# A mixture-of-experts loop: the down product with the inner rows stationary, and no transposes behind it

## What is computed

```python
E, K, H, F = (64, 6, 256, 96)
CAP = 2 * (2 * 128 * K // E)          # 48
...
buf = jnp.zeros((E, CAP + 1, H), x.dtype).at[se, slot].set(x[tok])[:, :CAP]
h = jax.nn.silu(jnp.einsum('ech,ehf->ecf', buf, w_gate)) * jnp.einsum('ech,ehf->ecf', buf, w_up)
out = jnp.einsum('ecf,efh->ech', h, w_down)
gathered = out[se, jnp.minimum(pos, CAP - 1)] * valid.astype(x.dtype)[:, None]
w = topk_w.reshape(-1)[order].astype(x.dtype)[:, None]
return jax.ops.segment_sum(gathered * w, tok, num_segments=Tn)
```

## Time and profile before

| | |
|---|---|
| three runs | 491.72, 495.5, 497.8 us (median 495.5) |
| the profiled execution | 492.98 us |
| its span in the trace | 491.0 us |
| mean granted PE clock | 0.921 of 2.4 GHz |
| expert loop in the trace, first `gate_up` to last scatter matmul | 179.12 to 304.96 us |

### The profile page before, as it was taken

The page is one execution under the profiler, slowest core; times in us unless marked ns, Lnnn a source line. Parts: engine busy times, 40 slices in busy tenths (PEclk is TensorE's granted clock), DMA queues, the critical chain, the costliest instruction groups (busy, mean ns, idle before and its releaser), DMA issues.

```text
span 491.0 us, 5331 instructions
## 1 busy us (share of the span) xinstructions
PE 417.0 (85%) x1778; PEld 245.5 (50%) x1778; DVE 374.3 (76%) x691; ACT 220.6 (45%) x411; POOL 96.0 (20%) x65
## 2 busy tenths in 40 slices
PE   0695999987970589999999999999999989998672
PEld 0241564576830246788888887544444434433220
DVE  4999788987799865988867785931796976739995
ACT  4464636382261355665666647152101104035880
POOL 0000000000000174222100000004768456541000
PEclk9998677998995698999999888799999999999897
DMA  7920000450067045667755332025000000000011
GB/s 285 418 97 0 2 0 0 159 217 0 1 211 259 21 116 141 184 202 224 229 194 180 131 116 75 2 116 226 0 1 1 0 0 1 1 0 1 0 44 43
DMA packets 12108, 47.85 MB, mean 97 GB/s; under 512 B 2881, under 2 KB 5290, under 8 KB 9650
## 3 DMA queue, kind: packets, MB, share of 16 engines
q1 hardware_dynamic: 10930, 43.58, 25.0%
q0 software_dynamic: 1152, 3.93, 3.2%
HBM read 45.14 MB, written 2.37 MB: 97 GB/s over the span
## 4 chain that ended last, share of the span: by engine, by line
PE 63%; DVE 24%; ACT 5%; DMA 3%; issue 3%; POOL 1%; SPq 1%; POOLq 0%; DVEq 0%; ACTq 0%
PE bank L1509 7%; PE bank L1649 7%; PE bank L1636 6%; PE bank L1561 6%; PE bank L1392 3%; PE bank L1681 3%; PE bank L1678 3%; DMA wrb<-in_w_router 3%; PE bank L1434 2%; PE bank L1542 2%; PE bank L1424 1%; PE bank L1570 1%; PE bank L1612 1%; PE bank L1701 1%; DVE arena L983 1%
## 5 line engine op out<-in xcount | busy, mean ns | idle before, releaser
L1509 PE MATMUL bank<-onehot,rows 128*128 128x512 f32 x192 | 54.1, 424 | 0.0
L646 ACT ACTIVATE early<-bank 128x512 f32<-128x512 f32 (+1 forms) x24 | 14.3, 597 | 86.0 <-PE bank L1649 76.6
L1202 DVE TENSOR_TENSOR early<-early,bank 128x512 f32<-128x512 f32 (+1 forms) x24 | 16.4, 685 | 39.1 <-ACT early L646 35.8
L1649 PE MATMUL bank<-arena 128*128 128x512 f32 (+1 forms) x96 | 42.2, 600 | 0.1
L375 POOL TENSOR_TENSOR early<-early,arena 128x512 f32<-128x512 f32 (+1 forms) x12 | 20.0, 1670 | 103.5 <-DMA arena<-pair_weights 96.6
L1636 PE MATMUL bank<-cT,arena 128*128 128x512 f32 x80 | 39.6, 622 | 0.0
L1509 PEld LDWEIGHTS bank<-onehot,rows 128*128 128x128 f32 x192 | 36.2, 201 | 6.3
L364 POOL DMA_INDIRECT arena<-token_rows,arena x24 | 28.6, 1191 | 37.3 <-DVE arena L1019 19.1
L1561 PEld LDWEIGHTS bank<-arena 96*128 96x128 f32 x256 | 30.7, 195 | 2.1 <-issue 1.0
L1027 DVE TENSOR_SCALAR onehot<-const,arena 128x1024 fp32r<-128x1024 f32 x24 | 17.9, 751 | 16.9 <-PE bank L1509 16.5
L1561 PE MATMUL bank<-arena 96*128 96x48 f32 x256 | 30.0, 275 | 0.0
(11 more groups left out here) (356 smaller groups left out, 908.7 us busy)
## 6 DMA issues: line engine op xcount, KB each, us to landing
arena<-in_w_gateup SPq DMA_DIRECT2D x16, 768.0 KB, 5.9
arena<-in_w_down SPq DMA_DIRECT2D x8, 768.0 KB, 8.6
const<-in_const SPq DMA_DIRECT2D x1, 2122.5 KB, 12.1
arena<-in_wq SPq DMA_DIRECT2D x1, 2048.0 KB
arena<-in_wo SPq DMA_DIRECT2D x1, 2048.0 KB, 8.0
arena<-in_w_upgate SPq DMA_DIRECT2D x1, 1408.0 KB, 6.0
kT<-in_kT SPq DMA_DIRECT2D x2, 512.0 KB, 5.2
xT<-in_xT SPq DMA_DIRECT2D x1, 1024.0 KB, 8.1
```

The costliest lines, as they stand in the source:

```text
L1509: return mm(bank[2 * ct + ch][:], rows1[:, i % RRING, part, ct * P:(ct + 1) * P], onehot1[:, t, ch * CHUNK:(ch + 1) * CHUNK], start=False, ...
L1649: last = mm(dst, (bup, bga)[z][:, f * P:f * P + fw], ((zu1, zg1), (zud, zgd))[k][z][:, ch * CHUNK:(ch + 1) * CHUNK], start=False, stop=Tru ...
```

## The change

In `down` the inner rows become the stationary operand and the weights move, 256 columns at once, so the result lies with the slots on partitions and `rows_out`, `outT1` and its copies go. A PSUM tile of 128 slots is two runs of 64 dense slots; each run touches two experts of 48 slots, and so takes two matmuls that accumulate. `h1` is laid out with 48 zero columns between experts, so that any window of 64 columns holds one expert's rows and zeros (`RUN_PIECE` lists expert and offset for the three runs of four experts). The zeros are written once by POOL. The rows come from banks 6 and 7. On PE two scatter matmuls stand before the first turn, and the rest in runs of 2, 4 and 16; the shared products stand at the three corresponding places of group 0, and group 0's `idle` products are gone. On ScalarE `euk(2)` comes before `rows_in(0)`. On DVE the two adds `num(3, ...)` move from group 7 to behind the last one-hot.

```diff
--- before.py
+++ after.py
@@ -52,6 +52,8 @@
 GT = GS // P
 ROW = C + E1
 HALF = P // 2
+RUN4 = 7 * CAP
+RUN_PIECE = ((0, 0), (1, CAP)), ((1, 2 * CAP + 16), (2, 3 * CAP + 16)), ((2, 4 * CAP + 32), (3, 5 * CAP + 32))
 XRING = 12
 RRING = 4
 LOW = -1e30
@@ -179,11 +181,12 @@
         hi2, mi2, lo2 = (at(o + 3072 + 128 * i, 64, 2) for i in range(3)); zrow = at(o + 3456, ROW, rows=1); o += XRING * ROW
         XW = GS + HALF - CAP
         xgT = [at(o + CT * XW * i, CT, XW) for i in range(2)]; ctok1 = at(o, NT, C); o += 2 * CT * XW
-        outT1, outw = at(o, CT, GS), at(o, GT, C); o += 768
+        outw = at(o, GT, C); o += 768
         shg = at(o, N, rows=F1)
         val1 = at(o + N, CHUNK); v96 = at(o + N + CHUNK, 2 * CAP, rows=E1); spreadv = at(o + N + CHUNK + 2 * CAP, GE, CAP, rows=E1)
         wsel = at(o + N, GT, E1); o += 2 * N
-        sg1, h1 = at(o, GE // 2, F1), at(o + GE // 2 * F1, GE, CAP, rows=F1); o += 2 * GS
+        sg1 = at(o, GE // 2, F1); o += GE // 2 * F1
+        h1 = at(o, 2 * CAP * GE - CAP, rows=F1); o += 2 * CAP * GE - CAP
         gw1 = at(4096, CT, E1, buf=arena2)
         wsg, wsu = at(4224, CT, F1, buf=arena2), at(4416, CT, F1, buf=arena2)
         wsd = at(4608, C, rows=F1, buf=arena2)
@@ -350,6 +353,7 @@
             pool.wait_ge(S("scatter0_done"), 4)
             pool.wait_ge(S("x1_ready"), 4)
             g.memset(zrow, 0.0).then_inc(S("zrow_ready"), 1)
+            g.memset(h1, 0.0).then_inc(S("pads_ready"), 1)
             pool.wait_ge(S("rows_out"), 48)
             for i in range(2):
                 last = g.memset(xgT[i][:, :, GS:XW], 0.0)
@@ -572,11 +576,11 @@
                 act.wait_ge(S("h1_turned"), 2 * g + j + 1)
                 if g >= 1:
                     act.wait_ge(S("ffn1_done"), g)
-                s.copy(h1[:, 4 * j:4 * j + 4, :], bank[4 + j][0:F1, 0:4 * HALF].rearrange("f (e c) -> f e c", c=HALF)[:, :, 0:CAP]
-                       ).then_inc(S("h1_ready"), 1)
-
+                s.copy(h1[:, RUN4 * j:RUN4 * j + 8 * CAP].rearrange("f (e c) -> f e c", c=2 * CAP)[:, :, 0:CAP],
+                       bank[4 + j][0:F1, 0:4 * HALF].rearrange("f (e c) -> f e c", c=HALF)[:, :, 0:CAP]).then_inc(S("h1_ready"), 1)
+
+            euk(2)
             rows_in(0)
-            euk(2)
             for g in range(NG):
                 hidden_silu(g, 0)
                 hidden_silu(g, 1)
@@ -597,18 +601,15 @@
                     euk(3)
                 if g == 5:
                     scaled(3, 1)
-                for ct in range(CT):
-                    act.wait_ge(S("ffn1_done"), g + 1)
-                    if g >= 1:
-                        act.wait_ge(S("rows1_ready"), GT * g)
-                    s.copy(outT1[:, ct, :], bank[6 + ct][:, 0:GS]).then_inc(S("outT_ready"), 1)
                 for t in range(GT):
                     i = g * GT + t
-                    act.wait_ge(S("outtr_done"), g + 1)
+                    act.wait_ge(S("ffn1_done"), g + 1)
                     act.wait_ge(S("wslot_ready"), g + 1)
+                    if g >= 1:
+                        act.wait_ge(S("rows1_ready"), i - GT + 1)
                     if i >= RRING:
                         act.wait_ge(S("scat1_done"), i - RRING + 1)
-                    row = bank[4 + t // 2][:, (t % 2) * C:(t % 2 + 1) * C]
+                    row = bank[6 + t // 2][:, (t % 2) * C:(t % 2 + 1) * C]
                     s.activation(rows1[:, i % RRING, 0, :], row, ACT.Copy, scale=wslot[:, i:i + 1])
                     s.activation(outw[:, t, :], row, ACT.Copy, scale=wslot[:, i:i + 1]).then_inc(S("outw_ready"), 1)
 
@@ -1078,8 +1079,6 @@
                 if g == 7:
                     num_own(3, 0)
                     num_own(3, 1)
-                    num(3, 0)
-                    num(3, 1)
 
                 for t in range(GT - 1):
                     slot_onehot(g, t)
@@ -1100,6 +1099,8 @@
                 if g == 6:
                     back_again(3, 1, 1)
             slot_onehot(NG - 1, GT - 1)
+            num(3, 0)
+            num(3, 1)
 
             dve.wait_ge(S("ratio_ready"), 2)
             for ct in range(CT):
@@ -1494,7 +1495,7 @@
                 if g == 0:
                     pe.wait_ge(S("shg_ready"), 2)
                 if g >= 2:
-                    pe.wait_ge(S("outT_ready"), 2 * (g - 1))
+                    pe.wait_ge(S("outw_ready"), GT * (g - 1))
                 for t in range(GT):
                     i = g * GT + t
                     for ct in range(CT):
@@ -1528,14 +1529,10 @@
                 pe.wait_ge(S(f"ring{g % 2}_in"), 48 * (g // 2 + 1))
                 pe.wait_ge(S("xgT_ready"), 2 * g + 2)
                 if g == 0:
-                    pe.wait_ge(S("pads_ready"), 1)
+                    pe.wait_ge(S("pads_ready"), 2)
                     pe.wait_ge(S("toki_ready"), 1)
                     pe.wait_ge(S("shg_ready"), 2)
-                else:
-                    pe.wait_ge(S("outw_ready"), GT * (g - 1) + 2)
                 for p in range(GE // 2):
-                    if g and p == GE // 4:
-                        pe.wait_ge(S("outw_ready"), GT * g)
                     for ct in range(CT):
                         for h in range(2):
                             e = 2 * p + h
@@ -1551,25 +1548,24 @@
                     last = tr(bank[4 + j][0:F1, q * P:(q + 1) * P], sg1[:, 2 * j + q, :], ident)
                 last.then_inc(S("h1_turned"), 1)
 
-            def down(g, half):
+            def down(g):
+
                 r = ring[g % 2]
-                pe.wait_ge(S("h1_ready"), 2 * g + half + 1)
                 if g < NG - 1:
                     pe.wait_ge(S("xgT_ready"), 2 * g + 4)
-                for e in range(half * GE // 2, (half + 1) * GE // 2):
-                    for ct in range(CT):
-                        last = mm(bank[6 + ct][:, e * CAP:(e + 1) * CAP], r["d"][:, e, ct * P:(ct + 1) * P],
-                                  h1[:, e, :], start=True, stop=True)
-                if half:
-                    last.then_inc(S("ffn1_done"), 1)
-
-            def rows_out(g):
-                pe.wait_ge(S("outT_ready"), 2 * g + 2)
+                else:
+                    pe.wait_ge(S("outw_ready"), GT * g)
                 for t in range(GT):
-                    for ct in range(CT):
-                        last = tr(bank[4 + t // 2][:, (t % 2) * C + ct * P:(t % 2) * C + (ct + 1) * P],
-                                  outT1[:, ct, t * P:(t + 1) * P], ident)
-                last.then_inc(S("outtr_done"), 1)
+                    if t < 2:
+                        pe.wait_ge(S("h1_ready"), 2 * g + t + 1)
+                    for i in range(2):
+                        for h in range(2):
+                            j, k = divmod(2 * t + h, GT)
+                            e, lo = RUN_PIECE[k][i]
+                            last = mm(bank[6 + t // 2][HALF * h:HALF * (h + 1), (t % 2) * C:(t % 2 + 1) * C],
+                                      h1[:, RUN4 * j + lo:RUN4 * j + lo + HALF], r["d"][:, 4 * j + e, :],
+                                      start=(i == 0), stop=(i == 1), skip_group_check=True)
+                last.then_inc(S("ffn1_done"), 1)
 
             idle(6, 2)
             rows_in(0)
@@ -1577,31 +1573,25 @@
             idle(3, 1)
             for g in range(NG):
                 gate_up(g)
+                if g:
+                    scatter_run(g - 1, 0, 2)
+                else:
+                    shared_down(1, 1)
                 turn_hidden(g, 0)
                 if g < NG - 1:
                     rows_in(g + 1)
                 if g:
-                    scatter_run(g - 1, 0, 2)
+                    scatter_run(g - 1, 2, 2)
                 else:
-                    shared_down(1, 1)
+                    shared_down(0, 0)
                 turn_hidden(g, 1)
                 if g:
-                    scatter_run(g - 1, 2, 4)
+                    scatter_run(g - 1, 4, 4)
                 else:
-                    shared_down(0, 0)
-                down(g, 0)
-                if not g:
                     shared_down(0, 1)
-                down(g, 1)
+                down(g)
                 if g:
-                    scatter_run(g - 1, 6, 6)
-                else:
-                    idle(4, 2)
-                rows_out(g)
-                if g:
-                    scatter_run(g - 1, 12, 12)
-                else:
-                    idle(6, 2)
+                    scatter_run(g - 1, 8, 16)
             for ct in range(CT):
                 for t in range(GT):
                     last = scatter(NG - 1, t, ct)
```

## The result

| kernel | executions | median us | range us |
|---|---|---|---|
| before, measured again beside after | 4 | 493.61 | 490.3 to 497.8 |
| after | 4 | 477.47 | 475.83 to 478.26 |

The account below looks back on a forecast made before the run. Inside the expert loop TensorE's own work was taken as the bound. Start -8.4 and clock +1.7, groups 2 to 6 -7.8, end -4.0 sum to -18.5: 492.98 becomes 474.5, rounded up to 475, range 469 to 484.

Parts of the forecast that it names:

- `down` at `gate_up`'s pace: New down in each group: takes gate_up's 2.82 us instead of 3.49, since both stream 3,072 columns in alternating halves.
- Rival 1: In down, the two column halves don't run side by side: 5.64 us per down, 497 us in all; chance 0.05.
- rival 2: At each down, entering and leaving the 64-column mode costs 0.35 us once or twice more: 480 us; chance 0.13.
- the bound: For down: twelve matmuls in one half take 5.64 us, two at a time 2.82, so nothing lies below.
- The steady group: An undisturbed group of the expert loop: 1.24 us saved by down and the transposes, 12.56 us instead of 13.80.
- rival 3: DVE becomes the bound, lagging up to 1 us in five groups of the loop: 479 us; chance 0.14.
- The clock: Lower-clock falls behind old downs, in groups 2 to 6 and behind the last, don't return; counted within -7.8 and -4.0.
- The end: From gate_up(7) to the last scatter matmul: 17.8 instead of 21.82 us, -4.0, the moved adds costing nothing.
- The start of the loop: Up to gate_up(2): -8.4 us from earlier down(0) and a removed wait, +1.7 for lower clock after a 2.5 us pause.
- the sentence on the transfers: Weight transfers into ring slots after each down: about 16 instead of 19 us available, still above the 8.6 of slower landings.

Follow-up runs that it names:

- halves_in_turn: Changed kernel with down's twelve matmuls reordered, all six of one column half before the six of the other; 485.07 us against 471.98 unaltered, one execution.
- shifted: Changed kernel with DVE's scans, adds and Newton steps of groups 0 to 4 set half a group later; 470.53 us, ratio 0.959 to the kernel before.
- before_again: The kernel before, unaltered, profiled once more; 486.42 us in one execution, median of before beside it 490.37.
- order_alone: The kernel before with its old down and transposes but everything else of the change (orders, shared products, euk, num); 490.95 us, ratio 1.001.
- again: The changed kernel run once more, unaltered; 472.2 us, ratio 0.963 to the kernel before.
- after_third: The changed kernel, unaltered, run again beside shifted; 471.98 us, ratio 0.963 to the kernel before.

## Why the prediction was right, and where it was not

- **`down` at `gate_up`'s pace**: forecast 2.82, measured 2.74 (2.65 where `gate_up` follows directly). `halves_in_turn` shows that the pace comes from the alternation. Rival 1 is out. So is rival 2: with 2.74 there is no room for another 0.35 us, although the mode is entered and left once more in each group. The drain that the Trainium skill (TensorEngine Tiling (Array Packing), Key Properties) states for a change of mode costs about 0.1 us here at most, by the difference between 2.74 and 2.65. No cost of the 96 contraction rows shows. What the prediction had slightly wrong is the bound: with 0.216 us for each pair of records twelve matmuls need 2.6 us, so something did lie below 2.82, and both in one half would be 5.2, not 5.64.
- **The steady group**: forecast 12.56, measured 12.49 (206.84 to 219.33). DVE was never late from group 2 on, so rival 3 is out; `shifted`, which moves work of DVE, has 12.49 there too.
- **The clock**: this is the term that was right in part by luck. The forecast said that the two falls behind the old `down` would not come again, and took them out of the time: 1.6 of the 8.6 us of groups 2 to 6 (70.99 against 69.37) and 2.7 of the 4.6 at the end (21.82 against 19.12). With the new `down` no such fall came in any of the eleven profiles. But `before_again` had none with the old one, while `order_alone` had lower clocks in groups 2 to 7 (0.87 at 275 to 280). The falls occur in some executions of the old `down` and not in others; that its 48 columns cause them was argued and isn't shown. That they go with the old `down` is likely (two of three profiles, against none of eleven), but no run shows what in it brings them. Without falls the change is worth 69.37 - 62.44 = 6.9 and 19.12 - 17.18 = 1.9, of which 0.4 each are short waits for DVE that the old kernel had; the whole loop is then 16.0 us shorter (121.50 in `before_again`, 105.49 in `again`) and not 18.5 or more.
- **The end**: 17.8 forecast, 17.18 measured; 40 scatter matmuls in one run took 9.21 us, 0.23 each and not 0.245. The adds moved behind the last one-hot cost nothing: PE has no wait there.
- **The start of the loop**: in `again` every step is as the forecast put it. `down(0)` at +6.62 (6.70), the chain from its end to the turn of group 1 5.86 (0.2 + 5.65), PE's pause 2.43 (2.5). From that turn to `gate_up(2)` are 10.74, of which 9.27 was the work; in `after_third` 10.16, of which 0.87 is the wait for weights and 9.29 the rest. The lower clock after the pause came in `again` (195 to 200 at 0.70) and not in `after_third`; where it came it cost 1.45 of the forecast's 1.7 us (10.74 against 9.29). In the execution that was profiled first, this whole term gave 0.4 instead of 6.7 us, because of the stop. That 475 came so close to 477.47 is therefore luck in part: 6.3 us were lost at the start, 1.4 more were won in groups 2 to 7 than forecast, and 1.7 came from an earlier start of the loop, which has nothing to do with the change (it starts at 177.4 to 181.2 us in the various profiles).
- **The sum in `again`**: -7.16 (25.87 against 33.03), -8.55 and -4.64, and +1.85 for a later start of the loop, give -18.5; 304.96 to 286.46 is 18.5.
- **The step that failed** is the sentence on the transfers: "about 16 instead of 19 us for them; that still exceeds the 8.6". The time available was right (15.5 us in `again`, from the request at 191.32 to `gate_up(2)` at 206.84). The 8.6 was a figure from a kernel in which the gathers are over when SP asks; there this very transfer took 8.7. The forecast itself moved `down(0)` 4 us forward and did not ask what the transfers would then meet. They met the gathers, and took 13.5 to 15. The margin that the forecast saw as 7 us was 2 in `again`, below nothing in `after_third`, where PE waited 0.9 us, and once DVE was out of the way the missing time took all that `shifted` should have gained.
- **Left out of the forecast**: that the new order and the new `down` need each other. Priced one at a time (the expectation for `order_alone`), the order was to bring 4 to 5 us by itself; it brought nothing.

## What to carry to other kernels

Where two operand shapes give the same product, count what the engine streams for each and what stands behind it: the small operand as stationary with the columns in two alternating halves ran `down` in 2.74 instead of 3.49 us, and gave the layout that the next step wanted, so that 0.57 us of transposes went too. Behind a wait that is removed, look for the next one before counting its whole length: a pause of 2.4 us for DVE hid a transfer that had next to no time left, and only with that transfer asked for earlier did the start of the loop win another 4 us (21.79 against 25.87), in the one profile that had no stop. A landing time holds for what runs beside the transfer: when a change moves a request, look at what it will then overlap (8.7 us behind the gathers, 13.5 to 15 among them), for even the same transfer's own time in the old trace does not tell. And ask for each part of a buffer when that part has been read.

## What the runs showed of the hardware

- Matmuls of 256 fp32 columns with 64-column stationaries, alternating between the column halves: twelve in 2.74 us. With all of one half first: 4.52 us. Records of one half start 0.216 us apart, those of the two halves run side by side.
- A 768 KB transfer, third of three: 8.7 to 9.5 us from issue to landing in five profiles where no gather was issued in the 7 us behind the request, 13.5 to 15.0 in four where two were issued within 2 us. In the middle of one of 14.9 us the DMA engines were as busy as before and behind it, but moved 209 to 257 GB/s instead of 361 to 393.
- Behind a pause of PE of 2 to 4 us the granted clock fell to 1.2 GHz in some executions and not in others of the same kernel (`again` and `after_third`, both 2.43 us). Without a pause it fell behind the old `down` in two of three profiles, and in none of eleven in groups 2 to 7 with the new one.
- In the four profiles with few semaphore events PE's semaphores moved later than its recorded matmuls end: by up to 5.2 us in the three with a stop, by up to 1.5 us in `before_again`. A recorded end of a matmul is a model; where an engine waits on PE for no visible reason, the semaphore's own time is what to read.
